# Down projection of a quantised decoder layer: four of eleven K tiles multiplied as integer codes, scaled after the product

## The reference, cut to what matters

```python
w[k,n] = q[k,n]*s[g,n] - (z[g,n]+1)*s[g,n]      # g = k // 128, q and z in 0..15
gate, up = x2 @ Wg, x2 @ Wu                     # 1024 x 1376
inter = gate * sigmoid(gate) * up
out = (inter @ Wd).astype(float16)              # K = 1376 (11 tiles of 128), 512 columns
x = layernorm(x + out)
```

## Time and profile before

| | us |
|---|---|
| median of 3 runs | 928.52 (928.19 to 930.88) |
| profiled execution, device time | 927.76 |
| its span, first to last instruction | 926.0 |
| TensorE busy | 878.3 (95%) |
| VectorE busy | 701.3 (76%) |
| ScalarE busy | 474.1 (51%) |
| GpSimd busy | 491.3 (53%) |
| mean granted clock of TensorE | 0.988 |

### The profile page before, as it was taken

How to read it: one execution, slowest core, us unless ns; L and a number is a source line. 1 busy time by engine, 2 the same in 40 slices (tenths; PEclk the granted TensorE clock), 3 DMA queues, 4 the chain that set the end, 5 groups by cost and what they waited for, 6 DMA issues and landing times.

```text
span 926.0 us, 17345 instructions
## 1 busy us (share of the span) xinstructions
PE 878.3 (95%) x6285; PEld 487.1 (53%) x6285; DVE 701.3 (76%) x1076; ACT 474.1 (51%) x1448; POOL 491.3 (53%) x430
## 2 busy tenths in 40 slices
PE   8888999889799999999999999999998899999997
PEld 3665777555445555555555555545544444444443
DVE  5688887887677888698797887997997545885333
ACT  4777878552555554565565565545655512333000
POOL 1264349526556676578567666768887411331011
PEclk9999999989999999999999999999999999999999
DMA  6754243320135412315234142134333120420001
GB/s 177 230 182 152 70 127 116 103 99 17 24 85 132 104 35 70 103 35 148 35 74 109 32 129 58 24 80 92 72 95 86 35 63 2 141 63 1 12 35 45
DMA packets 119173, 76.22 MB, mean 82 GB/s; under 512 B 72653, under 2 KB 103344, under 8 KB 119088
## 3 DMA queue, kind: packets, MB, share of 16 engines
q1 hardware_dynamic: 116784, 74.45, 30.6%
q10 hardware_dynamic: 2304, 0.66, 0.3%
HBM read 51.96 MB, written 6.36 MB: 63 GB/s over the span
## 4 chain that ended last, share of the span: by engine, by line
PE 58%; DVE 13%; POOL 9%; ACT 8%; issue 8%; DMA 4%; SPq 0%; ACTq 0%; DVEq 0%; POOLq 0%
PE bank L311 17%; PE bank L312 17%; PE bank L313 17%; POOL rot L569 3%; ACT prob L692 2%; DVE nmax L940 2%; POOL pn L586 2%; DVE rsin L1019 2%; POOL q2l L575 1%; DMA pT<-pn 1%; DVE pT L909 1%; ACT prob L834 1%; POOL deq L593 1%; ACT pT L643 1%; PE bank L1442 1%
## 5 line engine op out<-in xcount | busy, mean ns | idle before, releaser
L579 POOL TENSOR_TENSOR prob<-prob,rden 128x512 f32<-128x512 f32 x64 | 66.5, 1039 | 128.7 <-DVE rden L1084 128.6
L569 POOL TENSOR_TENSOR rot<-rcos,rsin 128x512 f32<-128x512 f32 x80 | 106.4, 1331 | 32.3 <-DVE rsin L1019 32.2
L311 PE MATMUL bank<-aTh,xqh 128*128 128x512 f16 x256 | 98.7, 386 | 5.0 <-DVE aTl L909 3.1
L312 PE MATMUL bank<-aTl,xqh 128*128 128x512 f16 x256 | 98.8, 386 | 0.0
L313 PE MATMUL bank<-aTh,xql 128*128 128x512 f16 x256 | 98.5, 385 | 0.0
L311 PE MATMUL bank<-xoh,o2h 128*128 128x512 f16 x256 | 98.3, 384 | 0.1
L312 PE MATMUL bank<-xol,o2h 128*128 128x512 f16 x256 | 98.2, 384 | 0.0
L313 PE MATMUL bank<-xoh,o2l 128*128 128x512 f16 x256 | 97.9, 383 | 0.0
L834 ACT ACTIVATE prob<-bank,ebias 128x128 f32<-128x128 f32 x256 | 90.4, 365 | 2.1
L1019 DVE SCALAR_TENSOR_TENSOR rsin<-bank,sinq 64x512 f32<-64x512 f32 x128 | 88.1, 688 | 1.7
L643 ACT ACTIVATE ebias<-nmax 128x4 f32<-128x4 f32 x128 | 26.9, 210 | 116.3 <-DVE nmax L1079 75.5
(11 more groups left out here) (181 smaller groups left out, 2528.3 us busy)
## 6 DMA issues: line engine op xcount, KB each, us to landing
tst<-tables SPq DMA_DIRECT2D x11, 768.0 KB, 6.2
xqs<-in_xwq SPq DMA_DIRECT2D x8, 1024.0 KB, 6.3
xos<-in_xwo SPq DMA_DIRECT2D x8, 1024.0 KB, 5.5
qst<-in_fq SPq DMA_DIRECT2D x11, 384.0 KB, 3.6
kstk<-stack SPq DMA_DIRECT2D x48, 64.0 KB, 2.3
qstk<-stack SPq DMA_DIRECT2D x21, 128.0 KB, 2.6
xs<-in_ctxT SPq DMA_DIRECT2D x2, 1024.0 KB, 8.1
res<-in_x SPq DMA_DIRECT2D x1, 2048.0 KB, 8.2
```

Of the source, the lines that this page charges most:

```text
L311: pe.matmul(out_ap, ah, bh, start=first, stop=False)
L312: pe.matmul(out_ap, ah, bl, start=False, stop=False)
L569: nc.gpsimd.tensor_tensor(rot[:, r % 2, :], rcos[:, r % 2, :], rsin[:, r % 2, :], ALU.add).then_inc(rope_rot, 1)
L579: nc.gpsimd.tensor_tensor(prob[:, v % 2, :].rearrange("p (h k) -> p h k", h=QH), prob[:, v % 2, :].rearrange("p (h k) -> p h k", h=QH), rd ...
```

## The change

Down tiles 7, 8, 9 and 10 are kept as integer codes, q - z - 1, exact in float16, so two matmuls (intermediate high and low part by the codes) do what three did. Each of these tiles has its own accumulation in a bank of its own, since its scale differs. VectorE multiplies each result by the scales, spread over the partitions by a DMA, into a float32 buffer `part`; GpSimd adds the four; `add_ffn` adds their sum to the bank of the other seven tiles. The eight code matmuls of batch b+1 are issued in the middle of batch b's other products (behind its third tile), those of batch 0 ahead of the loop. The other seven tiles of a batch now accumulate in bank 6 + b % 2, and the partial results go round banks 0 to 5. The scales of a code tile are loaded into the place of its former low part. For the four tiles the down block leaves `scale_codes`, `weights_hi` and `weights_lo`, and VectorE's subtraction is cut in two instructions. The diff, without the declarations of semaphores and tiles (`wdc` codes, `wds` scales, `part` 128 x 2 x 4 x 512 float32):

```diff
+DOWN_CODES = (7, 8, 9, 10)
+DOWN_SPLIT = tuple(i for i in range(NI) if i not in DOWN_CODES)
...
+        def part_bank(use):
+            return bank[(use + 4) % 6]
+
+        def split_before(i):
+            return sum(1 for k in DOWN_SPLIT if k < i)
...
+                if i - 2 in DOWN_CODES:
+                    sp.wait_ge(f_dcode, DOWN_CODES.index(i - 2) + 1)
                 sp.dma_start(qst[:, i % 2, :].rearrange("p (m n) -> p m n", m=3),
                              fq[i].rearrange("m p n -> p m n")).then_inc(codes_in[i % 2], 16)
                 sp.dma_start(tst[:, i % 2, :, :],
                              tables_d[:, 3 * i:3 * i + 3, :].rearrange("t m n -> t (m n)").partition_broadcast(P)).then_inc(codes_in[i % 2], 16)
+                if i in DOWN_CODES:
+                    sp.wait_ge(c_wo, STEPS)
+                    sp.dma_start(wds[i][:, :], tables_d[1, 3 * i + 2, :].partition_broadcast(P)).then_inc(scales_in, 16)
...
                     pool.wait_ge(f_wlo, i - 1)
-                    pool.wait_ge(f_dlo, i - 1)
-                nc.gpsimd.tensor_tensor(deq[:, i % 2, :], dif[:, i % 2, :], tst[:, i % 2, 1, :], ALU.mult).then_inc(f_deq, 1)
+                    pool.wait_ge(f_dlo, split_before(i - 1))
+                w = (2 if i in DOWN_CODES else 3) * D
+                nc.gpsimd.tensor_tensor(deq[:, i % 2, 0:w], dif[:, i % 2, 0:w], tst[:, i % 2, 1, 0:w], ALU.mult).then_inc(f_deq, 1)
+
+            def add_parts(b):
+                pairs = len(DOWN_CODES) // 2
+                for p in range(pairs):
+                    pool.wait_ge(f_part, len(DOWN_CODES) * b + 2 * p + 2)
+                    nc.gpsimd.tensor_tensor(part[:, b % 2, 2 * p, :], part[:, b % 2, 2 * p, :], part[:, b % 2, 2 * p + 1, :],
+                                            ALU.add).then_inc(f_pair, 1)
+                pool.wait_ge(f_pair, pairs * (b + 1))
+                nc.gpsimd.tensor_tensor(part[:, b % 2, 0, :], part[:, b % 2, 0, :], part[:, b % 2, 2, :], ALU.add).then_inc(f_parts, 1)
 
             def inverse_sd(e):
                 pool.wait_ge(ln_aggr, e + 1)
@@ -634,7 +663,10 @@
                 inverse_sds(0, t)
             for i in range(len(CODES_SLOT), NI):
                 scale_codes(i)
+            add_parts(0)
             for b in range(NB):
+                if b + 1 < NB:
+                    add_parts(b + 1)
                 inverse_sd(2 * NB + b)
...
-                nc.scalar.activation(wdh[i][:, :], deq[:, i % 2, 2 * D:], ACT.Copy).then_inc(f_whi, 1)
+                if i in DOWN_SPLIT:
+                    nc.scalar.activation(wdh[i][:, :], deq[:, i % 2, 2 * D:], ACT.Copy).then_inc(f_whi, 1)
...
-                nc.vector.tensor_tensor(dif[:, i % 2, :], nib[:, :], tst[:, i % 2, 0, :], ALU.subtract).then_inc(f_dif, 1)
+                w = (2 if i in DOWN_CODES else 3) * D
+                nc.vector.tensor_tensor(dif[:, i % 2, 0:w], nib[:, 0:w], tst[:, i % 2, 0, 0:w], ALU.subtract).then_inc(f_dif, 1)
+                if i in DOWN_CODES:
+                    nc.vector.tensor_tensor(wdc[i][:, :], nib[:, 2 * D:], tst[:, i % 2, 0, 2 * D:], ALU.subtract).then_inc(f_dcode, 1)
 
             def weights_lo(i):
-                dve.wait_ge(f_whi, 2 * i + 1)
+                dve.wait_ge(f_whi, i + split_before(i) + 1)
                 nc.vector.tensor_tensor(wgl[i % 4][:, :, :].rearrange("p m n -> p (m n)"), deq[:, i % 2, 0:2 * D],
                                         wgh[i % 4][:, :, :].rearrange("p m n -> p (m n)"), ALU.subtract).then_inc(f_wlo, 1)
-                dve.wait_ge(f_whi, 2 * i + 2)
-                nc.vector.tensor_tensor(wdl[i][:, :], deq[:, i % 2, 2 * D:], wdh[i][:, :], ALU.subtract).then_inc(f_dlo, 1)
+                if i in DOWN_SPLIT:
+                    dve.wait_ge(f_whi, i + split_before(i) + 2)
+                    nc.vector.tensor_tensor(wdl[i][:, :], deq[:, i % 2, 2 * D:], wdh[i][:, :], ALU.subtract).then_inc(f_dlo, 1)
...
+            def scale_part(b, e):
+                use = len(DOWN_CODES) * b + e
+                dve.wait_ge(f_yc, use + 1)
+                if use == 0:
+                    dve.wait_ge(scales_in, 16 * len(DOWN_CODES))
+                nc.vector.scalar_tensor_tensor(out=part[:, b % 2, e, :], in0=part_bank(use)[:, :], scalar=2.0 ** (-E_I - E_W),
+                                               in1=wds[DOWN_CODES[e]][:, :], op0=ALU.mult, op1=ALU.mult).then_inc(f_part, 1)
+
             def add_ffn(b):
                 dve.wait_ge(f_y, b + 1)
-                nc.vector.tensor_scalar(yh[:, b % 2, :], bank[4 + b % 4][:, :], 2.0 ** (-E_I - E_W), None,
-                                        ALU.mult).then_inc(f_y16, 1)
+                dve.wait_ge(f_parts, b + 1)
+                nc.vector.scalar_tensor_tensor(out=yh[:, b % 2, :], in0=bank[6 + b % 2][:, :], scalar=2.0 ** (-E_I - E_W),
+                                               in1=part[:, b % 2, 0, :], op0=ALU.mult, op1=ALU.add).then_inc(f_y16, 1)
                 dve.wait_ge(f_y16, b + 1)
                 nc.vector.tensor_tensor(res[:, b, :], res[:, b, :], yh[:, b % 2, :], ALU.add).then_inc(ln_sum, 1)
 
+            for b in range(2):
+                for e in range(len(DOWN_CODES)):
+                    scale_part(b, e)
             for b in range(NB):
                 add_ffn(b)
                 statistics(2, b)
+                if b + 2 < NB:
+                    for e in range(len(DOWN_CODES)):
+                        scale_part(b + 2, e)
                 normalised(2, b)
...
+            def down_codes(b):
+                if b % BH == 0:
+                    pe.wait_ge(f_ilo, GU_POS[(NI - 1, b // BH)] + 1)
+                if b == 0:
+                    pe.wait_ge(f_dcode, len(DOWN_CODES))
+                    pe.wait_ge(late_lo, BH)
+                for e, k in enumerate(DOWN_CODES):
+                    use = len(DOWN_CODES) * b + e
+                    if use in (2, 4):
+                        pe.wait_ge(f_inter, len(GATE_UP) - 2 + use // 2)
+                    if use >= 6:
+                        pe.wait_ge(f_part, use - 5)
+                    dst, ti = part_bank(use)[:, :], slice(b * S, (b + 1) * S)
+                    pe_.matmul(dst, inh[k][:, ti], wdc[k][:, :], start=True, stop=False)
+                    pe_.matmul(dst, inl[k][:, ti], wdc[k][:, :], start=False, stop=True).then_inc(f_yc, 1)
+
             def down(b):
-                pe.wait_ge(f_ilo, GU_POS[(NI - 1, b // BH)] + 1)
                 if b == 0:
-                    pe.wait_ge(f_dlo, NI)
-                    pe.wait_ge(late_lo, BH)
-                if b >= 4:
-                    pe.wait_ge(f_y16, b - 3)
-                for k in range(NI):
-                    last = split_products(pe_, bank[4 + b % 4][:, :], inh[k][:, b * S:(b + 1) * S], inl[k][:, b * S:(b + 1) * S],
-                                          wdh[k][:, :], wdl[k][:, :], k == 0, k == NI - 1)
+                    pe.wait_ge(f_dlo, len(DOWN_SPLIT))
+                if b >= 2:
+                    pe.wait_ge(f_y16, b - 1)
+                for k in DOWN_SPLIT:
+                    if k == DOWN_SPLIT[3] and b + 1 < NB:
+                        down_codes(b + 1)
+                    last = split_products(pe_, bank[6 + b % 2][:, :], inh[k][:, b * S:(b + 1) * S], inl[k][:, b * S:(b + 1) * S],
+                                          wdh[k][:, :], wdl[k][:, :], k == DOWN_SPLIT[0], k == DOWN_SPLIT[-1])
                 last.then_inc(f_y, 1)
...
             for n in range(len(GU_USE), len(GATE_UP)):
                 gate_up(n)
+            down_codes(0)
             for b in range(NB):
                 down(b)
```

More of the change, by code:

```diff
@@ L260, in decoder_kernel @@
         wd_at = (67, 77.5, 159.5, 87.5, 89.5, 91.5, 93.5, 95.5, 97.5, 107.5, 109.5)
-        wdh = [at(kb, f"wdh{i}", [P, D], F16) for i, kb in enumerate(wd_at)]
-        wdl = [at(kb + 1, f"wdl{i}", [P, D], F16) for i, kb in enumerate(wd_at)]
+        wdh = {i: at(wd_at[i], f"wdh{i}", [P, D], F16) for i in DOWN_SPLIT}
+        wdl = {i: at(wd_at[i] + 1, f"wdl{i}", [P, D], F16) for i in DOWN_SPLIT}
+        wdc = {i: at(wd_at[i], f"wdc{i}", [P, D], F16) for i in DOWN_CODES}
+        wds = {i: at(wd_at[i] + 1, f"wds{i}", [P, D], F16) for i in DOWN_CODES}
+        part = at(42, "part", [P, 2, len(DOWN_CODES), D], F32)
         in_at = (115.5, 119.5, 123.5, 127.5, 131.5, 135.5, 139.5, 143.5, 147.5, 151.5, 0)
@@ L307, in decoder_kernel @@
             sem("f_gate"), sem("f_up"), sem("f_gated"), sem("f_inter"), sem("f_ihi"), sem("f_ilo"))
+        f_dcode, scales_in, f_yc, f_part, f_pair, f_parts = (
+            sem("f_dcode"), sem("scales_in"), sem("f_yc"), sem("f_part"), sem("f_pair"), sem("f_parts"))
         f_y, f_y16, out_done = sem("f_y"), sem("f_y16"), sem("out_done")
```

## The result

| | before | after |
|---|---|---|
| median, us | 928.36 (927.87 to 930.88, 4 runs) | 921.9 (919.35 to 922.55, 4 runs) |
| ratio to before, 95% interval | | 0.992 (0.9894 to 0.9946) |
| profiled execution: time, span, us | 927.76, 926.0 | 919.35, 917.5 |
| matmuls | 6285 | 6253 |
| down stage, first product to last `yh`, us | 57.19 | 50.28 |

The change is 7.4 us faster by the ratio (5.0 to 9.8), which divides the mean times (921.4 by 928.9), and 6.5 by the two medians. The forecast was 6.7 us and 921.8 us. The profiled execution of the change is its fastest run, 8.5 us of span under that of before: 6.91 us of it lie in the down stage and 1.49 ahead of it, and this second piece is not from the mechanism forecast.

What follows compares the result with a forecast made beforehand. TensorE, busy throughout down, was taken as the bound: 926.0 - 6.91 for 32 matmuls + 0.2 for the tail = 919.3 us span, plus 1.76 outside and 0.76 for the median, 921.8 us; 8 in 10 range 921.0 to 926.0.

Steps and rivals of the forecast that it cites:

- TensorE's part: Down stage: 32 matmuls go, 32 x 0.2159 = 6.91 us; waits already met cost nothing.
- VectorE's part: Down stage: 32 added scalings fit; 5.9 us of a 6.26 us batch, slack 0.4, before holds.
- GpSimd's part: Down stage: 24 added additions; 5.0 us a batch, 6.0 with holds, close under 6.26.
- computed bound of 1.37 us for an addition: GpSimd in down: from an addition of about 1.37 us its load passes 6.26 us a batch.
- The rival that made this slower than before: GpSimd sets down's pace: unheld additions of 1.71 us, 7.3 us a batch, end at 929.7 us; chance 0.06.
- The holds: VectorE and GpSimd in down: `res` and `normalised` each held 0 to 1.27 us; VectorE 0.4 to 1.3 a batch.
- The tail: End of down: `normalised(6)` runs late and delays the last `yh`; 0.2 us taken.
- The weights: Gate/up, where down's weights are made: less VectorE work gives zero, TensorE being the bound; other end +0.5 us.
- The sum: Whole kernel: 926.0 - 6.91 + 0.2 = 919.3 us of span, 921.1 with 1.76 outside it, median 921.8.
- the low end of the range: Whole kernel time: 921.0 us, the lower end of the 8 in 10 range 921.0 to 926.0.
- the rivals: Other outcomes for down: small waits or partly covered pace 0.12, more holds 0.09, GpSimd's pace 0.06, clock 0.03.
- the clock rival: TensorE in down: bank waits restart it slow, some 2 us a batch, 14 us in all, 936 us; chance 0.03.

Runs made afterwards that it cites:

- e3: The changed kernel with a third matmul put back in each code tile, all else kept; ratio 1.0 to the kernel before, down stage 57.18 us.
- e4: The changed kernel with only tiles 9 and 10 as codes, one addition a batch; ratio 0.9962 to the kernel before, down stage 53.73 us.
- e8: The changed kernel with two more VectorE scalings in each of six batches, results unread; ratio 0.995 to the kernel before, down stage 52.74 us.
- e7: The changed kernel with a fourth GpSimd addition a batch, result unused; ratio 0.9966 to the kernel before, down stage 53.51 us.
- e9: The changed kernel with tile 6 as codes too, five code tiles; ratio 0.9975 to the kernel before, down stage 55.23 us.
- e2: The changed kernel run again, unchanged; ratio 0.9919 to the kernel before, down stage 50.28 us.
- e5: The changed kernel with a batch's code products ahead of its own other products, not in the batch before; ratio 1.0061 to the kernel before, stage 61.82 us.
- e1: The kernel before the change, run again unchanged; ratio 1.0002, down stage 57.18 us.

## Why the prediction was right or wrong

- **TensorE's part: right.** 6.91 us predicted, 6.91 in both profiles, and e3 and e4 put all of it on the matmuls. The last product starts 49.86 us behind the first, and no wait costs.
- **VectorE's part: right.** Four scalings take 2.45 us: 2.76 less the overlap of 0.08 us each that I gave them, which is there in full. The slack is 0.21 to 1.05 us, and none at the last `yh`, for a computed 0.4 less holds. Its 1.2 us more a batch in e8 were too much: `yh` came every 6.64 us in place of 6.26.
- **GpSimd's part: right, its load too high.** Unheld additions take 1.27 us. I computed 6.0 us a batch with 1.0 us of holds; its additions were stretched by 0.46 us a batch (4.26 us busy for three, against 3.80), and it still stands idle over 1 us a batch. That a pace of GpSimd's exists close above is shown by e7 and e9; the computed bound of 1.37 us for an addition was not tested. The rival that made this slower than before rested on unheld additions of 1.71 us; 16 of them have a median of 1.271.
- **The holds: right in kind, smaller in sum.** I expected one or two a batch. `res` is held in four batches of eight in earnest (1.34 to 1.56 us), `normalised` in none: GpSimd's second addition and `normalised` both become free when the last scaling ends (887.03), VectorE goes first, and the addition is the one that is held (1.47 us). A batch's holds on VectorE are 0.33 us on average, below my 0.4 to 1.3. VectorE is never late, though at the last `yh` it is just in time.
- **The tail: mis-sized.** I charged 0.2 us for `normalised(6)` running into the last `yh`. It takes 910.68 + 0.55 = 911.23, and `yh` starts at 911.22, 0.42 us behind the last product's start, as before: 0, in both profiles of the change. That is a tie, not a margin.
- **The weights: right.** `inl` does fall behind the scaling by GpSimd, 2.61 us in the line below, and `wgl` follows at once; TensorE doesn't notice. VectorE of the change while tile 10 is made:

```profile
832.00 0.42 DVE L1162 TENSOR_TENSOR wdc<-nib,tst 128x512 f16<-128x512 uint16 x1
832.33 2.61 DVE L1183 TENSOR_TENSOR inl<-gated,inh 128x512 f16<-128x512 f32 x1
834.87 1.21 DVE L1166 TENSOR_TENSOR wgl<-deq,wgh 128x1024 f16<-128x1024 f32 x1
```

- **The sum and the low end of the range: wrong.** The mechanism was right; what failed is the step from one profiled execution to a time with a range. "[T]hat for 8 in 10 is 921.0 to 926.0" left 0.8 us below the forecast. The ratio gives 928.36 x 0.992 = 920.9 and e2 gives 928.42 x 0.9919 = 920.9, both just below it, with single runs down to 919.35. The median itself, 921.9, lies inside and next to the forecast; that is in part the luck of four runs, since e2's median is 920.59. Two terms of the sum show why. The tail's 0.2 us measured 0: without it the forecast is 921.6 and the saving 6.9 us. And "926.0", with 0.76 us on top for the median, stood for everything ahead of 862.4 as if it were fixed; in eleven profiles that point moves over 3.7 us. Half of that below 921.6 is 919.8, about where a range that allowed for it would have begun (an estimate). I had put all the width on the side of the rivals, none of which happened. (The range of 921.2 to 922.7 for a saving of 6 to 7 us doesn't follow either: 928.52 less these is 921.5 to 922.5.) The 0.5 us between the 6.9 us of the stage and the 7.4 of the ratio is far inside the interval of 5.0 to 9.8, and no run tells whether it is more than this spread.

Of the clock rival, e5 shows more than the change could: three real stalls of 1.2 us left the clock at 1.00, so a stall alone does not bring the 0.59 of the earlier trace rows. At 196 us, behind idle stretches that were alike, the clock showed 0.50 in e1 and 1.00 in e2; so what a stall costs differs from one execution to the next. The rival's own price was also too high: 12 matmuls at 0.2159 us are 2.6 of the 4.2 us, so 1.6 us was lost there and not 2, which makes 932.9 and not 936.

## What to carry to other kernels

When one engine is busy throughout a stage, count the starts it loses and multiply by the pitch of starts: that was exact here for the stage. For the whole time, first see how far the stage's begin moves from one execution to the next, and let the range allow for it on both sides. Then compute the period of each engine that takes over work, with the mutual holds, and compare it with the new, shorter period of the first: the first 32 scalings and 24 additions were free, and the next eight of each cost more than the eight matmuls gave (e9). Work that passes through two other engines had to be issued a whole period ahead here; the same instructions one batch later in the list turned a gain of 7 us into a loss of 6 (e5).

## What the runs showed of the hardware that was not expected

- A hold between VectorE and GpSimd settles into a pattern: in the change `res` is held in every other batch and comes first in the others (1.34, 0.69, 1.34, 0.69 us, the same in both of its profiles). The timelines read as if a held addition shifted the next meeting; that was not tested.
- The same kernel had the same stretch at two clocks: from 196 to 200 us TensorE's granted clock is 0.69 in the first profile of the change and 1.00 in the second. In all eleven profiles the reciprocal at 204 to 207 us waits 0.68 to 0.91 us for TensorE where the clock was 0.50 from 198 to 200 us, and does not wait where it was 0.88 and more.
- Together with the hold of `xvl` behind it, this goes with 1.7 us of the whole execution at that point, in programs that are the same up to there. Neither the clock nor the hold was changed on purpose in a run.
